# A recommendation kernel's start and fill: row numbers in two loads, F ahead of the look-ups, VectorE's work in another order

## What is computed

```python
e = stack([tbl_f[ids[:, f]] for f in range(26)], axis=1)      # [512, 26, 32]
x1 = einsum('bik,bjk,hij->bhk', e, e, W1) + b1[None, :, None]  # 128 maps
x2 = einsum('bik,bjk,hij->bhk', x1, e, W2) + b2[None, :, None]
z = sum(concatenate([x1, x2], axis=1), axis=-1)                # [512, 256]
h = maximum(concatenate([z, dense_ctx], axis=1) @ W_top1 + b_top1, 0)
h = maximum(h @ W_top2 + b_top2, 0)
y = h @ W_top3                                                 # [512, 1]
```

## Time and profile before

| | us |
|---|---|
| median of 3 runs | 256.03 (255.72 to 256.58) |
| the profiled execution | 255.76 |
| its span, first to last instruction | 253.8 |
| TensorE busy | 147.2 (58%) |
| VectorE busy | 107.4 (42%) |
| ScalarE busy | 88.3 (35%) |
| GpSimd busy | 85.4 (34%) |
| mean granted TensorE clock | 0.798 of 2.4 GHz |

### The profile page before, as it was taken

The page is one execution under the profiler, slowest core; times in us unless marked ns, Lnnn a source line. Parts: engine busy times, 40 slices in busy tenths (PEclk is TensorE's granted clock), DMA queues, the critical chain, the costliest instruction groups (busy, mean ns, idle before and its releaser), DMA issues.

```text
span 253.8 us, 3289 instructions
## 1 busy us (share of the span) xinstructions
PE 147.2 (58%) x1169; PEld 129.5 (51%) x1169; DVE 107.4 (42%) x397; ACT 88.3 (35%) x295; POOL 85.4 (34%) x96
## 2 busy tenths in 40 slices
PE   0784001300003243020058999999999999999995
PEld 0772001000001131000034899998999899989994
DVE  6940019100000003000049998992589458945401
ACT  2540001000010401040037779857447744774112
POOL 3877777777777777771000000000000000000000
PEclk9999555555555586555558999999999999999999
DMA  6650000000010100000000020100000000000000
GB/s 193 230 109 13 13 14 14 13 13 13 13 13 14 18 13 13 13 13 5 0 0 0 0 87 0 21 0 4 0 15 7 3 0 15 6 0 3 12 9 2
DMA packets 7350, 5.86 MB, mean 23 GB/s; under 512 B 3473, under 2 KB 6805, under 8 KB 7206
## 3 DMA queue, kind: packets, MB, share of 16 engines
q1 hardware_dynamic: 4230, 3.86, 5.1%
q0 software_dynamic: 2816, 1.45, 3.9%
q10 hardware_dynamic: 288, 0.35, 0.5%
HBM read 5.18 MB, written 0.00 MB: 20 GB/s over the span
## 4 chain that ended last, share of the span: by engine, by line
PE 46%; another core or an unknown queue 29%; issue 12%; ACT 8%; DMA 3%; SPq 0%; ACTq 0%
PE p_zh L888 12%; PE p_t L868 12%; PE p_t L876 7%; DMA region<-in_L_rec_W 3%; ACT e_diag L325 3%; PE p_x L930 3%; PE p_t L843 2%; PE p_zh L843 2%; PE p_zh L896 2%; PE p_t L828 1%; ACT region L416 1%; PE p_x L888 1%; PE p_x L941 1%; PE p_t L960 1%
## 5 line engine op out<-in xcount | busy, mean ns | idle before, releaser
L303 POOL DMA_INDIRECT rows<-in_tbl,idx x88 | 84.5, 960 | 29.3 <-issue 26.5
L843 PE MATMUL p_zh<-S,region 128*128 128x352 f32 (+1 forms) x26 | 13.2, 641 | 54.6 <-issue 29.5
L843 PE MATMUL p_t<-S,region 128*128 128x352 f32 (+1 forms) x26 | 14.4, 682 | 40.9 <-ACT region L416 22.3
L630 DVE TENSOR_TENSOR region<-region 128x14 f32<-128x14 f32 (+10 forms) x11 | 2.9, 303 | 81.0 <-issue 51.1
L843 PEld LDWEIGHTS p_zh<-S,region 128*128 128x128 f32 x26 | 6.2, 257 | 60.7 <-issue 60.1
L843 PEld LDWEIGHTS p_t<-S,region 128*128 128x128 f32 x26 | 6.2, 262 | 47.5 <-issue 46.8
L888 PE MATMUL p_zh<-region 124*128 124x128 f32 x256 | 29.6, 277 | 0.0
L888 PEld LDWEIGHTS p_zh<-region 124*128 124x128 f32 x256 | 28.9, 192 | 0.5
L325 ACT COPY e_diag<-eT 32x160 f32<-32x160 f32 (+2 forms) x80 | 28.6, 358 | 0.8
L333 ACT COPY region<-p_t 124x352 f32<-124x352 f32 x32 | 14.5, 452 | 20.6 <-PE p_t L868 19.8
L760 DVE COPY L<-p_t 74x208 f32<-74x208 f32 x24 | 8.9, 371 | 22.8 <-PE p_t L876 22.8
(11 more groups left out here) (118 smaller groups left out, 249.8 us busy)
## 6 DMA issues: line engine op xcount, KB each, us to landing
region<-in_L_rec_W SPq DMA_DIRECT2D x1, 1664.0 KB
rows<-in_tbl,idx POOLq DMA_INDIRECT x88
wt<-in_W_top SPq DMA_DIRECT2D x1, 512.0 KB
region<-in_W_top SPq DMA_DIRECT2D x1, 512.0 KB
region<-in_tbl SPq DMA_DIRECT2D x4, 125.0 KB
w<-in_L_rec_W ACTq DMA_DIRECT2D x1, 338.0 KB, 3.3
gmix<-L SPq DMA_DIRECT2D x4, 56.0 KB
gmix<-L SPq DMA_DIRECT2D x4, 30.0 KB
```

What stands on the lines that cost most here:

```text
L303: pool.indirect_dma_start(rows[:, t, f * EMB:(f + 1) * EMB], None, tables[f], bass.IndirectOffsetOnAxis(ap=idx[:, t, f:f + 1], axis=0),).t ...
L843: last = nc.tensor.matmul(p_f[n % 2][:, j1 - 1 - j, 0:width], w2T[:, j, :], S[:, 0:width], start=True, stop=True)
```

## The change

It does these things:

- **Row numbers**: SP loads tile 0's alone; the rest of them come from ScalarE's queue behind W1. GpSimd waits for the first part, and for the rest ahead of tile 1. VectorE's `split_rows` waits for both.
- **Start**: ScalarE zeroes e_diag[0] from a column of zeros that GpSimd makes; VectorE zeroes e_diag[1] at the start instead of e_diag[0], and not again later. W1's symmetric sum is made in halves, ahead of `split_rows`. `first_weights` stands behind one_hot(0) instead of one_hot(3).
- **F**: slice 0 comes ahead of look_up(0), the dense products behind slice 1; look_up(2) behind slice 7 and look_up(3) behind slice 11. The first turn of tile 0 no longer waits for F; its second half does.
- **ScalarE** does spread(0,1) behind slice 5 instead of 4; spread(0,3) and spread(0,4) are VectorE's.
- **VectorE**: choose(1) ahead of group(0,2), choose(2) behind middle_first, choose(3) behind the saves of WT, tile 1's first two `rows_to_columns` and the ones of e_diag[1] in pieces between the sums of F. For tiles 2 and 3, `rows_to_columns` of group 0 and six of its nine products come behind turns 3 to 6 of the tile before.
- **z of tile 0** waits for WT bank by bank, and for the last look-up only ahead of z's first half.
- **Last tile**: h1 in four banks, saved by ScalarE and VectorE in turn, h2 by halves, y copied by VectorE.

Cut to its core:

```diff
@@ sync, gpsimd, scalar
-            sp.dma_start(idx[:, :, :], ids.rearrange("(p t) f -> p t f", t=TILES)).then_inc(ids_in, 16)
+            sp.dma_start(idx[:, 0, :], ids.rearrange("(p t) f -> p t f", t=TILES)[:, 0, :]).then_inc(ids_in, 16)
...
+                if t == 1:
+                    pool.wait_ge(ids_rest_in, 16)
...
+            act.dma_start(idx[:, 1:TILES, :], ids.rearrange("(p t) f -> p t f", t=TILES)[:, 1:TILES, :]).then_inc(ids_rest_in, 16)
...
+            nc.scalar.copy(e_diag[0].rearrange("p s q c -> p (s q c)"),
+                           zero[:, :].to_broadcast([P, STEPS * QUADS * COLS])).then_inc(diag_zero[0], 1)
...
-                if n == 4:
+                if n == 5:
                     spread(0, 1)
                 if n == 9:
                     spread(0, 2)
-                if n == 13:
-                    spread(0, 3)
-            spread(0, 4)
@@ vector
+            first_sums(0, FIELDS // 2)
...
+            first_sums(FIELDS // 2, FIELDS)
+            first_diagonal()
             split_rows()
...
+            choose(1)
             group(0, 2)
             for m in reversed(range(A, 20)):
                 high_pairs(m)
-            diag_zeros(1)
             group(0, 3)
+            spread(0, 3)
             group(0, 4)
-            choose(1)
+            spread(0, 4)
...
             middle_first()
+            choose(2)
...
-            diag_ones(1)
-            choose(2)
-            choose(3)
...
+                    if t < LAST:
+                        if k == 3:
+                            rows_to_columns(t + 1, 0)
+                        if k == 4:
+                            products(t + 1, 0, 0, 2)
...
@@ tensor
-            look_up(0)
-            pe.wait_ge(hot_ready, 2 * TILES)
...
                 if n == 0:
+                    look_up(0)
+                if n == 1:
                     pe.wait_ge(dense_in, 16)
...
-            look_up(2)
-            pe.wait_ge(f_saved, len(SLICES) - 1)
-            look_up(3)
+                if n == 7:
+                    pe.wait_ge(chosen_ready, 2)
+                    look_up(2)
+                if n == 11:
+                    look_up(3)
...
+                if n == 0:
+                    pe.wait_ge(f_saved, len(SLICES))
```

194 lines of the change are left out of this document (115 added, 79 removed).

## The result

| | median us | runs | |
|---|---|---|---|
| before | 255.88 | 4 | 255.58 to 256.58 |
| after | 260.36 | 4 | 259.37 to 260.48 |
| after / before | 1.0163 | | 95% interval 1.013 to 1.0196 |

The changed kernel is 1.6% slower, 4.5 us, where 2.8 us less was forecast. Its profiled run took 260.28 us with a span of 258.5 (before: 255.76 and 253.8). Some executions of a kernel are slower than its others (of the kernel before, most executions in the last two groups of experiments: 260.0 to 261.8 us, where its others took 255.0 to 256.1), and comparisons here use the faster ones alone.

The account below looks back on a forecast made before the run. GpSimd's gathers with TensorE's results seen late (the lag) bound it until the release at about 128.8 us, then TensorE's chain. Gains 0.7 + 1.7 + 0.4 = 2.8 gave a 253.2 us median; range 248.0 to 257.0.

Parts of the forecast that it names:

- Start and gathers: GpSimd's first gathers: W1's sum in halves blocks them for less time; gain 0.7 us, bounds 1.2 to -0.2.
- The smaller load: At the start, row numbers may land a little sooner; counted as nothing, since a gather under the memset waits anyway.
- Lagging stage: First stage, TensorE's results seen some 20 us late: products change order, not sum; slice 4 again seen at about 109.8.
- rival (c): First stage: look_up(0), now behind slice 0, pays the lateness in full; 16.2 us later, 269 us; chance 0.15.
- Release: End of TensorE's late results, about 128.8 us, 13.3 us after GpSimd's last gather; all the rest counts from it.
- TensorE behind the release: After 128.8 us, look-ups 2 and 3 fill waits among F's slices before the first turn; gain 1.7 us.
- VectorE behind the release: VectorE's chain from choose(1) to the sums W's transposes need: 24.25 and 1.6 us, ready at 154.7, 0.9 in hand.
- Rival (b): VectorE is the bound, its sums for W's transposes ready behind turn 7; 255.2 us with 1.5 too much; chance 0.11.
- Tiles 1 to 3: VectorE's next-tile work behind turns 3 to 6 fills its idle time while TensorE sums z; worth 0.
- Tail: Last tile: h1 and h2 in halves on ScalarE and VectorE, y copied by VectorE; gain 0.4 us.

Follow-up runs that it names:

- e3c: The changed kernel with the row numbers in one load again, run with the lag (TensorE's results read late); 256.81 us in one execution.
- v6: The kernel before with only VectorE's work for the next tile between the turns added, run with the lag; 255.52 us, 0.999 of before.
- e2c: The kernel before with 12 extra bf16 products ahead of W2's transposes, run with the lag; 255.44 us in one execution.
- v1c: The changed kernel with look_up(0) ahead of slice 0 of F again, run with the lag; 257.58 us in one execution.
- c2: The kernel before with VectorE's next-tile work between turns and the last tile's h1, h2, y in halves; 255.34 and 255.61 us, and four times 259.3 to 260.3.
- e1c: The kernel before with VectorE's copies into S right behind the first tile's one-hot, run with the lag; 256.28 us in one execution.

## Why the prediction was wrong, step by step

**Start and gathers: right in the mechanism, and the size in part by luck.** 0.7 was forecast, 0.58 came. The second gather takes 1.52 and the third 0.95 us where before the third took 2.17: each half of W1's sum catches less than the whole did, and that is worth 0.65 up to the fourth gather. The first gather also starts 0.20 sooner (4.25 against 4.45), which the prediction set to nothing, since a gather under the memset would wait for its end. It takes 1.11 us against 1.10, and the 0.20 stays. 0.27 is lost again over the other 84 gathers.

**The smaller load: counted as nothing, and it was not.** The prediction looked at GpSimd's wait only. VectorE waits for the rest of the numbers too (split_rows stands behind both): it started at 7.77 instead of 5.99, and TensorE's selectors at 8.58 instead of 6.96. "VectorE's two orders of work before 16 us end alike" was true of the work and false of the wait: they end at 15.54 and 16.52. Without the lag W2's landing covers most of it; with the lag it is the likeliest of the moved things to make the lag catch W2's transposes: e3c gets 3.5 us back (256.81 against 260.28), and in the table W2's last copy goes with the start on the row numbers. One execution does not settle it, and one load alone does not bring back before's late begin (35.81 against 15.67 for W2's last copy).

**Lagging stage: the step that failed.** "Their order changes, their sum does not" took the lag for a tax on a fixed list of products that ends at look_up(1). It is a stretch between two times. Its end is set by the gathers, as assumed; its beginning is at about 12 to 16 us and wanders, and whatever TensorE issues before that is free. In the profile of before this was all 26 transposes of W2 and half of look_up(0), a thing that the 2.7 us per look-up product had shown and that rival (c) named. In after most of the transposes pay as well: 38.8 us from 11.76 to 50.56, where before took 4.4 (11.24 to 15.67), a term that stood in no sum. The line of products up to slice 4 no longer fits between the ends, and 7.9 us of work lie behind the release instead of ahead of it. What moved the beginning stays open.

**Rival (c): the right mechanism, with two wrong numbers.** It let only look_up(0) pay, 16 us, and it let the release wait for the line, 269. What paid was more (look_up(0) is read 64 us later), and the release did not wait: what is not through at 128.3 is simply done behind it without the lag, 7.9 us for three slices and a look-up. So the price is not the lateness but the work left over. The sign given for this rival, choose(1) read at 134 or later, came: it is read at 135.60.

**Release: right time, wrong law.** 128.8 less 0.6 or 0.7 was forecast, 128.3 seen. But "13.3 us behind the last gather" is 6.2 with half the gathers.

**TensorE behind the release: not borne out in its size.** From slice 7 to the first turn it is 12.8 us against 15.9, where 1.7 less was forecast. The look-ups do fill waits, and that is worth 0.8; the other 2.4 is the granted clock, 1.00 there since slice 7 comes 8 us later, and it is paid for ahead of slice 7. What the new order would gain with slice 7 at the release, as the forecast had it, no run shows.

**VectorE behind the release: right in its length.** From choose(1) to the last sum it is 26.1 us (135.60 to 161.70) where 25.85 was forecast (24.25 and 1.6); of it the eight e_diag copies take 1.88 (1.6 taken). It starts at look-up 1's end, 6.8 us behind the forecast's 128.8, so VectorE's chain is about as late as TensorE's. TensorE wants the last sum at 162.36: 0.66 in hand where 0.9 was forecast, and W's transposes follow the eighth turn without a gap. Rival (b) did not happen; its own time, 1.5 us too much, is 254.7 (253.2 and 1.5) and not the 255.2 that stands there.

**Tiles 1 to 3: right with the lag** (v6: 0.999), incomplete without it, where the last tile of before came 1.8 us late (27.21 less 25.45) behind a wait for gathered rows. **Tail: right.** From the last tile's z sums to the end 15.16 to 14.76 us with the lag, 0.4 for 0.4.

So most parts were sound beside the failed step, and one, the 1.7 us, was not tested. Without the lag the changed kernel is 2.6 us faster; the 4.5 us are lost with it.

## What to carry to other kernels

When a stage waits for results that come late, ask when the lateness begins as well as when it ends, count everything that the engine has issued ahead of the beginning as free, and ask what becomes of it if the start moves by 2 us. A cost per item that differs between two items of one kind (2.7 and 5.4 here) is evidence of such an edge, not noise. And in a stretch that ends at a time set elsewhere, lateness costs nothing until a unit of work falls behind the end; then it costs that unit's own time, not the lateness.

## What the hardware showed that was not expected

The same program took 256 and 154 us on the same kind of chip, in one group with TensorE's results read up to 71 us after their products were issued (the dense ones of the changed kernel, 56.91 to 128.28), in the other without. Behind W2's transposes each late record of TensorE takes some 2.8 us until it is seen (look_up(0): 16 records from 56.17 to 101.06, 44.9 us; two records of a slice of one field 5.6, from 50.56 to 56.17); among the transposes themselves it is less at first (a bank of four is read 5.0 us behind the bank ahead of it, later 7.8, 7.7 and 9.8). Most of GpSimd's gathers take 0.94 or 0.95 us either way. The lateness ends with them and after a delay that was 6.2 us for 44 of them and 13.4 for 88.

What in the chip delays the results, why some groups of runs are free of it, and what starts it between 12 and 16 us was not found. TensorE's higher rate is ruled out as the start (e3c: late before the rate rose; e2c: in time for 2 us after it), and so is the order of look_up(0) and slice 0 (v1c). VectorE's copies into S are not needed for it: c2 has them 4 us later than e1c and is as late. Not tried in the kernel before are ScalarE's zeroing, W1's sum ahead of the row numbers, and a later start of VectorE. Every execution here was profiled, and no run tells whether the lag is there without the profiler.
